# Two passes over destinations in a graph kernel: maximum and scalar lookups as bf16 products, row scaling moved to another engine

## The reference

```python
def _conv_layer(x, he_attr, row, col, stoich, W, att, bias):
    xt = x @ W
    et = he_attr @ W
    a = xt[row] @ att[:H] + et[col] @ att[H:]
    a = leaky_relu(a, 0.2)
    amax = segment_max(a, col)
    ex = exp(a - amax[col]);  den = segment_sum(ex, col);  alpha = ex / den[col]
    B = segment_sum(abs(stoich), col);  Binv = where(B > 0, 1 / B, 0)
    eout = segment_sum((Binv[col] * stoich * alpha)[:, None] * xt[row], col)
    ...                      # then the same way back, by row
```

## Time and profile before

| what | value |
|---|---|
| timed runs (3), median | 14665.91 us (14642.43 to 14757.12) |
| span of the profiled execution | 11822.6 us |
| own time of the profiled execution | not recorded beside the span |
| median less span | 2843.3 us |
| busy share of the span | PE 69%, DVE 69%, POOL 65%, ACT 43% |
| mean granted TensorE clock | 0.691 of full speed |
| POOL indirect gathers in all passes (L615 twice, L1454) | 4640 + 928 + 1856 |

### The profile page before, as it was taken

One profiled execution on the slowest core, in us unless ns is written; L12 is line 12 of the kernel. 1 busy time (PEld: TensorE's weight loads), 2 busy tenths in 40 slices (PEclk: granted clock), 3 DMA queues, 4 the chain that ended last, 5 costly groups with the idle time before them and its releaser, 6 DMA issues. The chain is left out here.

```text
span 11822.6 us, 182142 instructions
## 1 busy us (share of the span) xinstructions
PE 8182.0 (69%) x47949; PEld 6566.7 (56%) x47949; DVE 8126.2 (69%) x31101; ACT 5076.1 (43%) x14757; POOL 7702.8 (65%) x7673
## 2 busy tenths in 40 slices
PE   7895777666656777555545555788886677767776
PEld 5675777544436777444434554666665444545554
DVE  9765888655556777655562222688887788878888
ACT  4553444322224444222231111466665566646665
POOL 2445777677766777677757777355653677747775
PEclk8876666655556667666567677899998666556566
DMA  1112222355542222578844444344443444434443
GB/s 17 9 20 55 53 53 53 74 130 130 128 110 60 53 53 53 134 203 205 205 131 130 132 131 128 101 145 146 147 146 100 132 134 134 133 105 134 133 134 114
DMA packets 712736, 1297.08 MB, mean 110 GB/s; under 512 B 196563, under 2 KB 369073, under 8 KB 711217
## 3 DMA queue, kind: packets, MB, share of 16 engines
q0 software_dynamic: 282368, 575.57, 22.4%
q1 hardware_dynamic: 388992, 615.05, 16.6%
q10 hardware_dynamic: 40368, 94.82, 2.1%
HBM read 1050.01 MB, written 234.74 MB: 109 GB/s over the span
## 5 line engine op out<-in xcount | busy, mean ns | idle before, releaser
L615 POOL DMA_INDIRECT WK<-tab,IDX x4640 | 4624.3, 997 | 1688.7 <-issue 1345.2
L1454 POOL DMA_INDIRECT B<-tab,IDX x1856 | 1774.7, 956 | 848.5 <-issue 507.3
L615 POOL DMA_INDIRECT H<-tab,IDX x928 | 878.9, 947 | 644.1 <-DVE H L1260 346.4
L1473 DVE TENSOR_REDUCE WK<-PS 128x4 f32<-128x1024 f32 x928 | 1130.4, 1219 | 190.9 <-PE PS L1599 188.6
L1584 ACT ACTIVATE B<-B 128x33 f32<-128x33 f32 x5568 | 1211.2, 308 | 8.0
L839 ACT ACTIVATE WK<-WK 128x128 f32<-128x128 f32 x1856 | 592.6, 390 | 1289.5 <-DMA WK<-tab,IDX 1265.9
L921 PE MATMUL PS<-WK 128*128 128x129 f32 x3712 | 744.2, 362 | 429.6 <-DVE WK L974 208.8
L1632 PEld LDWEIGHTS PS<-B,H 128*128 128x128 f32 x3712 | 819.8, 330 | 283.0 <-issue 274.3
L1632 PE MATMUL PS<-B,H 128*128 128x132 f32 x3712 | 880.7, 430 | 87.3 <-DVE ACC L1486 87.3
L921 PEld LDWEIGHTS PS<-WK 128*128 128x128 f32 x3712 | 638.3, 259 | 527.1 <-DVE WK L974 268.0
L921 PE MATMUL PS<-WK,B 128*128 128x129 f32 x3712 | 829.1, 394 | 12.1 <-ACT WK L1160 8.5
(11 more groups left out here) (426 smaller groups left out, 19037.9 us busy)
## 6 DMA issues: line engine op xcount, KB each, us to landing
H<-onehots SPq DMA_DIRECT2D x232, 768.0 KB
B<-onehots SPq DMA_DIRECT2D x232, 384.0 KB
onehots<-B ACTq DMA_DIRECT2D x232, 384.0 KB
WK<-tab,IDX POOLq DMA_INDIRECT x4640
onehots<-WK SPq DMA_DIRECT2D x232, 256.0 KB
B<-onehots SPq DMA_DIRECT2D x232, 256.0 KB
WK<-onehots SPq DMA_DIRECT2D x232, 256.0 KB
onehots<-B SPq DMA_DIRECT2D x232, 128.0 KB
```

Of the source, the lines that this page charges most:

```text
L615: po.indirect_dma_start(out=G[:, g % n, k, :], out_offset=None, in_=table, in_offset=bass.IndirectOffsetOnAxis(ap=IDX[:, idx, t:t + 1], ax ...
L1454: po.indirect_dma_start(out=eG[:, g % 4, k, :], out_offset=None, in_=tab[TW3], in_offset=bass.IndirectOffsetOnAxis(ap=IDX[:, o, t:t + 1], ...
L1473: ve.tensor_reduce(eM2[:, g, b:b + 2, 2 * i:2 * i + 2, 1] if isinstance(g, int) else eM2[:, bass.ds(g, 1), b:b + 2, 2 * i:2 * i + 2, 1].re ...
```

## The change

For each group of pass a:

- `tab` holds the logit also as three bf16 numbers that add up to it (columns 260 to 262 of a row in bf16). The destination's place is put in bits: one product of the transposed one-hot with a table of 18 columns (`BITA`) gives bits and complements, and four small products add the three logit parts of the gathered rows (L933, L936). ACT reads the 18 x 512 result (L879), and one product with `SELA` (L911) gives the masked logits in the layout that the maximum wants. The steps L833, L839 and L876 are gone.
- The block's scalar and maximum go back to the edges as bf16 parts: the four products (L926) are bf16 with six columns and not fp32 with two; a reduce on DVE adds the parts. DVE has casts and subtractions that split the maximum into parts.
- The scaling of rows moves from DVE (L799) to ACT: an exponential and four copies with a scale (L889, L891). The column of weights is written only when l = 0.
- Lags are longer by one: the last step of DVE is at lag 9. The one-hot on DVE now waits for `S.ag` of the group eight earlier. The wait for the gather moves from ACT at lag 1 to PE at lag 2.
- `l0_ve` has four more DVE steps in each of 13 items, and `bits_ve` and `pick_pe` make the constants once.

```diff
-        fa = [[WK[:, 0:7900], 0], [B2[:, 200:NB * 260], 0]]
-        aG, aOH, aVA, aXR, aOT = room(fa, 8, 4, TW), room(fa, 8, 4, 128), room(fa, NT), room(fa, 4, 4, 128), room(fa, 4, 512)
-        aN1, aR = room(fa, 512), room(fa, 2, 4, 133)
-        aTM, aE, aLR, aOLD, aT2 = room(fa, 2), room(fa, 4), room(fa, 4), room(fa, 2, 2), room(fa, 2, 2)
-        aY, aDD, aEX, aEW, aNB = room(fa, 2, 2, 3), room(fa, 8, 6), room(fa, 8, 6), room(fa, 2, 4), room(fa, 1)
-        aSF = B2[:, 0:NB * 2]
-        as2 = PS[:, 5, 0:8].rearrange("p (k c) -> p k c", c=2)
+        fa = [[WK[:, 0:8540], 0], [B2[:, 300:NB * 260], 0]]
+        aG, aOH, aVA, aOT = room(fa, 8, 4, TW), room(fa, 8, 4, 128), room(fa, NT), room(fa, 8, 256)
+        aET, aR = room(fa, 2, 256), room(fa, 2, 4, 133)
+        aTM, aE, aLR, aL, aT2 = room(fa, 2), room(fa, 4), room(fa, 4), room(fa, 2, 2), room(fa, 2, 2)
+        aST, aD1, aS2 = room(fa, 2, 2, 8), room(fa, 2), room(fa, 4, 2)
+        aDD, aEX, aEW = room(fa, 8, 6), room(fa, 8, 6), room(fa, 2, 4)
+        aGb = aG.rearrange("p a b c -> p (a b c)").bitcast(BF16).rearrange("p (a b c) -> p a b c", a=8, b=4)
+        aOTb = aOT.rearrange("p a b -> p (a b)").bitcast(BF16).rearrange("p (a b) -> p a b", a=8)
+        aETb = aET[0:18].rearrange("p a b -> p (a b)").bitcast(BF16).rearrange("p (a b) -> p a b", a=2)
+        aSTb = aST.rearrange("p a b c -> p (a b c)").bitcast(BF16).rearrange("p (a b c) -> p a b c", a=2, b=2)
+        aSTm = aSTb[:, :, :, 0:8].rearrange("p a b (c s) -> p a b c s", s=4)[:, :, :, :, 0:3]
+        aSF = B2[:, 0:NB * 6]
+        aSFb = aSF.bitcast(BF16).rearrange("p (b c) -> p b c", c=12)
+        SF = aSF.rearrange("p (b c) -> p b c", c=6)[:, :, 4:6]
+        as2 = PS[:, 5, 0:24].rearrange("p (k c s) -> p k c s", c=2, s=3)
...
-                    ve.tensor_tensor(aE, aG[:, re_, :, 128], as2[:, :, 0], ALU.add).then_inc(S.e1, 1)
+                    ve.tensor_reduce(aS2.rearrange("p k c -> p (k c)"), as2.rearrange("p k c s -> p (k c) s"), AX.X,
+                                     ALU.add).then_inc(S.sv, 1)
...
-                    ve.tensor_copy(aOLD[:, 0, 0:1], mx)
-                    ve.tensor_copy(aY[:, qm, 0, 1:2], aSF[:, bass.ds(vm[0] * 2, 1)])
-                    ve.tensor_tensor(mx, mx, aTM[:, 0:1], ALU.max).then_inc(S.m1, 1)
+                    ve.wait_ge(S.ns, at.ns + gm)
+                    ve.wait_ge(S.s2, at.s2 + gm - 1)
+                    ve.wait_ge(S.mx, at.mx + gm)
+                    ve.tensor_copy(aST[:, qm, 0, 0:6], aSF[:, bass.ds(vm[0] * 6, 6)]).then_inc(S.m1, 1)
...
-                    ve.tensor_tensor(aR[:, qw, :, 0:128], aG[:, rw, :, 0:128],
-                                     aEW[:, qw, :].unsqueeze(2).broadcast_to([128, 4, 128]), ALU.mult).then_inc(S.r, 1)
...
+                    ve.wait_ge(S.ag, at.ag + gf - 7)
+                    ve.tensor_tensor(aOH[:, rf, :, :], io4, low(0, gf), ALU.is_equal).then_inc(S.oh, 1)
...
+                    ve.tensor_copy(aSTb[:, qm, :, 4], aL[:, :, 1]).then_inc(S.z, 1)
+                    ve.tensor_tensor(aDD[:, rm, 4:6], aL[:, :, 0], aL[:, :, 1], ALU.subtract).then_inc(S.m5, 1)
+                    ve.wait_ge(S.z, at.z + gm + 1)
+                    ve.tensor_tensor(aD1, aL[:, :, 1], aSTb[:, qm, :, 4], ALU.subtract).then_inc(S.gp, 1)
+                    ve.wait_ge(S.gp, at.gp + gm + 1)
+                    ve.tensor_copy(aSTb[:, qm, :, 5], aD1).then_inc(S.gl, 1)
+                    ve.wait_ge(S.gl, at.gl + gm + 1)
+                    ve.tensor_tensor(aSTb[:, qm, :, 6], aD1, aSTb[:, qm, :, 5], ALU.subtract).then_inc(S.ns, 1)
...
         def a_ac(ac, p):
             at, ring = raised_before(p)
@@ -828,28 +869,31 @@
             def body(j, u):
                 if f := turn(j, u, 1):
                     g, r = f
-                    ac.wait_ge(S.oh, at.oh + g + 1)
-                    ac.wait_ge(S.xr, at.xr + g)
-                    ac.activation(aN1, aOH[:, r, :, :].rearrange("p k n -> p (k n)"), ACT.Identity, bias=aNB,
-                                  scale=BIG).then_inc(S.n1, 1)
-                    ac.wait_ge(s_ring[r], landed(g, r, 8, ring[r]))
-                    ac.wait_ge(S.xt, at.xt + g - 3)
-                    ac.wait_ge(S.n1, at.n1 + g + 1)
-                    for k in range(4):
-                        i = ac.activation(aXR[:, r % 4, k, :], aN1[:, 128 * k:128 * k + 128], ACT.Identity,
-                                          bias=aG[:, r, k, 128:129])
-                    i.then_inc(S.xr, 1)
                     ac.wait_ge(S.pt, at.pt + g + 1)
-                    ac.wait_ge(S.s2, at.s2 + g - 3)
-                    ac.activation(aOT[:, r % 4, :], PS[:, 4, 0:256].bitcast(BF16), ACT.Copy).then_inc(S.ot, 1)
-                if f := turn(j, u, 5):
+                    ac.wait_ge(S.s2, at.s2 + g - 7)
+                    ac.activation(aOTb[:, r, :], PS[:, 4, 0:256].bitcast(BF16), ACT.Copy).then_inc(S.ot, 1)
+                if f := turn(j, u, 2):
+                    g, r = f
+                    ac.wait_ge(S.xr, at.xr + g + 1)
+                    ac.wait_ge(S.xt, at.xt + g - 1)
+                    ac.activation(aETb[:, r % 2, :], PS[0:18, 2 + r % 2, :], ACT.Identity, bias=abi[0:18, :],
+                                  scale=asc[0:18, :]).then_inc(S.n1, 1)
+                if f := turn(j, u, 6):
                     g, r = f
                     ac.wait_ge(S.p2, at.p2 + g + 1)
                     ac.activation(aEX[:, r, :], aDD[:, r, :], ACT.Exp).then_inc(S.ex, 1)
+                if f := turn(j, u, 7):
+                    g, r = f
+                    ac.wait_ge(S.p3, at.p3 + g + 1)
+                    ac.wait_ge(S.ag, at.ag + g - 1)
+                    ac.activation(aR[:, r % 2, :, 128], aDD[:, r, 0:4], ACT.Exp)
+                    for k in range(4):
+                        i = ac.activation(aR[:, r % 2, k, 0:128], aG[:, r, k, 0:128], ACT.Copy, scale=aEW[:, r % 2, k:k + 1])
+                    i.then_inc(S.r, 1)
             meet(ac)
-            sweep(5, body)
-
-        def a_pe(pe, p):
+            sweep(7, body)
+
+        def a_pe(pe, p, l):
             at, ring = raised_before(p)
 
             def body(j, u):
@@ -860,31 +904,40 @@
                     for k in range(4):
                         t = pe.transpose(PS[:, 4, 64 * k:64 * k + 64].bitcast(BF16), upper(aOH)[:, r, k, :], identb)
                     t.then_inc(S.pt, 1)
-                if f := turn(j, u, 7):
+                if f := turn(j, u, 3):
+                    g, r = f
+                    pe.wait_ge(S.n1, at.n1 + g + 1)
+                    pe.wait_ge(S.tm, at.tm + g - 1)
+                    pe.matmul(PS[:, r % 2, :], SELA, aETb[:, r % 2, :], start=True, stop=True).then_inc(S.xt, 1)
+                if f := turn(j, u, 8):
                     g, r = f
                     pe.wait_ge(S.r, at.r + g + 1)
                     pe.wait_ge(S.xb, at.xb + g - 1)
+                    n = 129 if l else 130
                     for k in range(4):
-                        mm = pe.matmul(aAG(r, k // 2), aOH[:, r, k, :], aR[:, r % 2, k, 0:130], start=k % 2 == 0,
+                        mm = pe.matmul(aAG(r, k // 2)[:, 0:n], aOH[:, r, k, :], aR[:, r % 2, k, 0:n], start=k % 2 == 0,
                                        stop=k % 2 == 1)
                     mm.then_inc(S.ag, 1)
+                if f := turn(j, u, 5):
+                    g, r = f
+                    pe.wait_ge(S.ns, at.ns + g + 1)
+                    pe.wait_ge(S.sv, at.sv + g)
+                    for k in range(4):
+                        mm = pe.matmul(as2[:, k, :, :], aOTb[:, r, 128 * k:128 * k + 128],
+                                       aSTm[:, r % 2, k // 2, :, :], start=True, stop=True)
+                    mm.then_inc(S.s2, 1)
                 if f := turn(j, u, 2):
                     g, r = f
-                    pe.wait_ge(S.xr, at.xr + g + 1)
-                    pe.wait_ge(S.tm, at.tm + g - 1)
+                    pe.wait_ge(S.ot, at.ot + g + 1)
+                    pe.wait_ge(S.n1, at.n1 + g - 1)
+                    pe.matmul(PS[0:18, 2 + r % 2, :], BITA, aOTb[:, r, :], start=True, stop=False)
+                    pe.wait_ge(s_ring[r], landed(g, r, 8, ring[r]))
                     for k in range(4):
-                        t = pe.transpose(PS[:, r % 2, 128 * k:128 * k + 128], aXR[:, r % 4, k, :], ident[:, :])
-                    t.then_inc(S.xt, 1)
-                if f := turn(j, u, 4):
-                    g, r = f
-                    pe.wait_ge(S.ns, at.ns + g + 1)
-                    pe.wait_ge(S.e3, at.e3 + g)
-                    for k in range(4):
-                        mm = pe.matmul(as2[:, k, :], aOT[:, r % 4, 128 * k:128 * k + 128], aY[:, r % 2, k // 2, 1:3],
-                                       start=True, stop=True)
-                    mm.then_inc(S.s2, 1)
+                        t = pe.matmul(PS[0:3, 2 + r % 2, 128 * k:128 * k + 128], aGb[:, r, k, 260:263], identb, start=False,
```

(9 more changed lines are left out.)

85 lines of the change are left out of this document (54 added, 31 removed).

## The result

| | us |
|---|---|
| before, median of 5 runs | 14665.91 (14601.87 to 14757.12) |
| changed kernel, median of 5 runs | 14791.86 (14738.81 to 14819.18) |
| ratio | 1.0082, 95% interval 1.0056 to 1.0108 |
| profiled execution of the changed kernel | span 14817.4, own time 14819.18 |

The change costs about 120 us. The time lies within the predicted range and within the 1% that I called "no change", but the interval excludes no change, and the forecast of +19 on the median was too low by 107 us.

The account below looks back on a forecast made before the run. POOL's indirect gathers were taken to bound pass a, at 5.22 us a group. On 14665.9 us, +14 us in passes a and +12 us once made +26, weighed to 14685 us; range for 8 in 10: 14590 to 14840.

Parts of the forecast that it names:

- The sum made on the span, the rest constant: Whole kernel: priced on the profile's 11822.6 us span; the other 2843.3 us of the timed median taken as constant.
- under POOL's cover: Passes a: POOL's gathers pace iterations, 5.22 us a group, so work removed from ACT, PE and DVE is worth nothing.
- Rival 3: Timed runs unlike the profile, engines the bound: 0.5 us less work a group gives -232 us, 14446; chance 0.08.
- The gain from fewer colliding gathers: POOL in pass a: one two-SBUF-input DVE step fewer shortens gathers, 0.10 us a group, 24 us a pass.
- The loop between ACT and PE: Pass a: L936 releases L879, then exponentials, scalings, L918, back to L936; 5.58 us at 1.2 GHz, 4.21 at 2.4.
- the term of +14 us: Passes a: 5.25 us a group forecast against 5.22 before, +0.03 over 464 groups.
- Rival 1: Pass a: the ACT-PE cycle becomes the bound, +0.29 to +0.48 us a group, 14813 to 14900; chance 0.22.
- What would show it: Profile signs in pass a: if the cycle binds, POOL's gather waits for L891 over 0.3 us, L918 some 2 us.
- The one-hot's wait for `S.ag`: DVE in pass a: only steps PE wants an iteration later stand behind it, so no cost was given.
- Once-costs: Outside the group loop: l0_ve items, block scalars, constants and drain, together +12 us, between +8 and +30.
- The sum: Whole kernel: +14 us in passes a and +12 us once make +26 us; with the kept clock weighed, 14685 us.

Follow-up runs that it names:

- experiments 2: Changed kernel with the scaling of rows put back on VectorE (DVE): 14624.85 us, 0.9996 of the kernel before.
- 6: Changed kernel with ACT's scaling and exponential moved ahead of L879: 14682.28 us, 1.0002 of the kernel before.
- Experiments 3: Changed kernel with PE's L933 and L936 moved ahead of L918: 14693 us, 1.0053 of the kernel before.
- second profiles: Both kernels, unedited, profiled again beside each other on one chip: before 14617.64 us, changed kernel 14753.89 us.
- experiment 4: Changed kernel with VectorE's one-hot L847 and its wait for S.ag moved behind the split tail: 14752.96 us, 1.0087 of the kernel before.
- (5): Changed kernel with pass a's gathers cut to 64 of 128 rows, all but the first 8 groups: 14774.91 us, 1.0097 of the kernel before.
- (9): Changed kernel with eight more 128x1 copies on ACT behind L874 in each iteration of passes a: 14768.49 us, 1.0067 of the kernel before.

## Why the prediction was right, and where it was wrong

**The sum made on the span, the rest constant: wrong.** This is the step that failed first. The 2843 us were stands in the very passes, so that groups took 6.6 us (1540/232), not 5.22, and POOL, busy 59% of the pass, didn't set its length. All prices "under POOL's cover" were made in a kernel that isn't the timed one. Rival 3 named this case and drew the wrong sign from it: that the engines' work would then count, -232 us. What counts when engines stand is the order in which signals are waited for, and the removed work of PE (85 to 103 us a pass) bought nothing that shows: with the scaling back on VectorE the kernel is level with the one before.

**The gain from fewer colliding gathers: right in size, worth nothing.** I took 24 us a pass; 22.5 came (986 to 962 ns). It can be undone and doubled without effect on the time: with the scaling on VectorE a gather takes 1012 ns and the two passes are 84 and 60 us shorter, with half the rows 926 ns and they are no shorter.

**The loop between ACT and PE: its terms right, its effect mis-sized.** From L879 at 1515.24 to L879 at 1520.60 it is 5.36 us, where I had 5.58 for the low clock; the scaling 1.26 (1.28 forecast), L879 0.68 to the next step (0.67), L936 0.63 (0.59), L918 1.90 to the next step (1.84). The granted clock is 0.60, as forecast. But the loop sets the time only of every second group: 5.36 us there, against the 5.02 of four gathers. In the other group ACT stands 6 us for a held signal, which the prediction didn't know of. So the term of +14 us came out at 63 + 57 = 120 us, 0.26 us a group. Rival 1 had the place and the direction, "L879 behind L936, scaling behind L879", and nearly the size, 0.29 to 0.48 us a group. That it is the place is shown by experiments 2 and 6: the scaling elsewhere, or ahead of L879, and the kernel is level with the one before. How the place costs is shown in part. Experiments 3 and 6 each break the loop in another way, and each takes the 0.3 us off every second group, 32 us a pass. In the kernel before such groups took 5.33 us on the mean of the first pass and 5.22 of the second, with its slower gathers, and in the changed kernel 5.36 and 5.35 (second profiles): here the loop used up what the faster gathers gave, about as forecast. The groups that end in a long stand went from 8.26 and 8.21 us to 8.57 and 8.56. The long stands are 368 us of the first pass before, 424 after and 327 with the scaling on VectorE; they go with where the scaling is, but by what way isn't shown.

**What would show it.** The text said: POOL's gather then waits for ACT's L891 for over 0.3 us at a time. It does, for 3.8 us on the mean, but the kernel before stands as often and nearly as long for VectorE's scaling (104 x 3.54), so the sign doesn't tell the loop from the held signals. The loop's own mark is the 0.64 us at 1523.00. It also said PE's L918 would wait for L891 2 us an iteration; it waits 0.76 us in the cycle above, since PE is held at L911 first.

**The one-hot's wait for `S.ag`: right.** Costed at nothing, it is nothing (experiment 4), though VectorE stands 415 us there.

**Once-costs: within the bounds, nearly twice the sum.** 12 us forecast, 8 to 30 as bounds; 21 found (12.5 + 2.4 + 8.8 - 2.7), which in part is the drain. The item of `l0_ve` hardly grew, since PE had kept VectorE waiting there. After, against the 1.33 us of the earlier trace rows, an item starts 1.37 us behind the last, 986.71 less 985.34:

```profile
985.34 0.17 DVE L1815 CAST WK<-PS 128x4 bf16<-128x4 f32 x1 [0.98 <-PE PS L1715]
985.55 0.70 DVE L1816 COPY WK<-PS 128x516 f32<-128x516 f32 x1
986.16 0.15 DVE L1817 TENSOR_TENSOR WK<-PS,WK 128x4 f32<-128x4 f32 x1
...
986.71 0.16 DVE L1815 CAST WK<-PS 128x4 bf16<-128x4 f32 x1
```

**The sum** came within range in part by luck. The list of edits was sound and one rival knew the place, but every price was made for a POOL that sets the pace and an execution without held signals, and the forecast change, +19 us, is about a sixth of the measured one. What kept the time in range is that the loss stayed small beside a range of 250 us.

**What stays open.** Why signals of PE are held until a run of gathers has landed, why the execution read before the prediction shows none of it in pass a, why the long stands are longer in the changed kernel, and why pacing POOL helps beyond shortening the runs. The experiments bear on it only so far: it isn't the amount of data (5), nor the number of ACT's instructions (9). Fewer or other signals on the landings weren't tried, nor was pacing in passes b to e, in which POOL stands over 1 us too (46 to 173 times a pass in the kernel before's second profile). Whether the recording of an execution has a part in them can't be told from recorded executions; that the traces with stands hold a third of the semaphore updates of the one without fits it, and fits merged signals as well.

## What to carry to other kernels

Compare the span of the profile with the timed runs before pricing anything: if they differ by 20%, the profile shows another regime, and covers read from it don't hold. When a step is moved to an engine that "has time", look at what stands ahead of it in that engine's order: a step that everyone waits for shouldn't stand behind a wait that it doesn't need (scaling ahead of L879: 1.0002 in place of 1.0067 to 1.0082 of the kernel before, at no cost). And a producer that runs in bursts can be worth slowing down: one wait more on POOL made the changed kernel 0.4% faster than the kernel before. Last, when an engine seems to act late on a signal, look up when the signal itself was recorded.
